# A fused Mamba2 and mixture-of-experts block: decays exponentiated in SBUF, channel tiles on alternating PSUM banks, output weights one slot sooner, a reordered end

## The reference

```
xn = layernorm(x)                                     # x: 1 x 1024 x 512
proj = xn @ in_proj_w.T                               # gate 8192 | hBC 10240 | dt 128
hBC  = silu(causal_conv4(hBC) + conv_b)               # hs 8192 | B 8 x 128 | C 8 x 128
dt   = clip(softplus(dt + dt_bias), 0, 100); A = -exp(A_log)
# 128 heads of 64 channels, 8 chunks of 128 tokens, A_cum = cumsum(dt * A) in a chunk
L    = exp(segsum(dt * A))                            # 128 x 128 lower triangle, a head and a chunk
Y_diag = (C B^T * L) @ (hs * dt)                      # inside a chunk
state  = decay * state + B^T @ (decay_states * hs * dt)
Y_off  = (C @ previous state) * exp(A_cum)
g    = (Y_diag + Y_off + hs * D) * silu(gate)
out  = (g * rsqrt(mean(g * g, group of 1024) + 1e-5) * norm_w) @ out_proj_w.T
result = x + out + x @ base_W.T + LoRA experts (top 2 of 8 by softmax)
```

## Time and profile before

| | |
|---|---|
| median of 3 runs | 1668.06 us (1667.99 to 1668.83) |
| profiled execution | 1670.87 us, span 1669.3 us |
| mean granted TensorE clock | 0.991 |
| busy, TensorE matmuls | 1616.3 us |
| busy, VectorE / ScalarE / POOL | 1366.4 / 1243.0 / 1327.1 us |

### The profile page before, as it was taken

How to read it: one execution, slowest core, us unless ns; L and a number is a source line. 1 busy time by engine, 2 the same in 40 slices (tenths; PEclk the granted TensorE clock), 3 DMA queues, 4 the chain that set the end, 5 groups by cost and what they waited for, 6 DMA issues and landing times.

```text
span 1669.3 us, 31876 instructions
## 1 busy us (share of the span) xinstructions
PE 1616.3 (97%) x10792; PEld 1308.9 (78%) x10792; DVE 1366.4 (82%) x1675; ACT 1243.0 (74%) x2625; POOL 1327.1 (80%) x1238
## 2 busy tenths in 40 slices
PE   7989999999999999999999999999999999999998
PEld 5777887878788787878878787887878788787776
DVE  5868789877888888887888888888788877888777
ACT  5267787777778687777878778787777878777774
POOL 3147689987889778896899868998788977999886
PEclk9999999999999999999999999999999999999999
DMA  3153365454544554445545446554554446544453
GB/s 125 58 201 103 113 179 166 147 158 126 163 145 127 159 155 138 127 133 149 172 144 151 125 117 181 145 144 137 156 159 121 140 131 183 150 125 133 128 146 101
DMA packets 216401, 236.11 MB, mean 141 GB/s; under 512 B 154280, under 2 KB 155824, under 8 KB 212016
## 3 DMA queue, kind: packets, MB, share of 16 engines
q1 hardware_dynamic: 216240, 234.08, 48.1%
HBM read 147.52 MB, written 55.05 MB: 121 GB/s over the span
## 4 chain that ended last, share of the span: by engine, by line
PE 82%; DVE 8%; issue 4%; ACT 4%; POOL 2%; DMA 1%; ACTq 0%; DVEq 0%; SPq 0%; POOLq 0%
PE P L262 9%; PE P L264 9%; PE P L263 9%; PE P L499 8%; PE P L363 6%; PE P L339 6%; PE P L340 6%; PE P L356 6%; PE P L346 6%; PE P L357 6%; PE P L370 4%; DVE OL L836 3%; ACT OH L795 1%; PE P L489 1%; PE P L486 1%
## 5 line engine op out<-in xcount | busy, mean ns | idle before, releaser
L595 ACT ACTIVATE P<-AB,SC 128x128 f32<-128x128 f32 x1016 | 307.1, 362 | 25.3 <-DVE EM L926 25.1
L262 PE MATMUL P<-xh,AH 128*128 128x512 f32 x656 | 262.5, 400 | 3.5 <-DVE xl L957 2.9
L264 PE MATMUL P<-xh,AL 128*128 128x512 f32 x656 | 256.7, 391 | 0.0
L263 PE MATMUL P<-xl,AH 128*128 128x512 f32 x656 | 256.1, 390 | 0.0
L813 DVE SCALAR_TENSOR_TENSOR hsX<-P,cwt,hsX 128x1023 f32<-128x1023 f32 x189 | 241.8, 1279 | 13.1 <-ACT hsX L532 8.6
L339 PE MATMUL P<-GH,xh 128*128 128x512 f32 x512 | 215.3, 421 | 0.0
L356 PE MATMUL P<-OH,gTh 128*128 128x512 f32 x512 | 201.4, 393 | 2.9 <-issue 2.7
L340 PE MATMUL P<-GH,xl 128*128 128x512 f32 x512 | 203.6, 398 | 0.0
L357 PE MATMUL P<-OH,gTl 128*128 128x512 f32 x512 | 200.1, 391 | 0.0
L1249 POOL TENSOR_TENSOR al<-al,dhs 128x512 f32<-128x512 f32 x64 | 97.4, 1522 | 113.2 <-DVE al L1093 113.2
L926 DVE TENSOR_TENSOR EM<-P,Gt 128x1024 f32<-128x1024 f32 x127 | 154.7, 1218 | 23.6 <-issue 22.1
(11 more groups left out here) (223 smaller groups left out, 4158.7 us busy)
## 6 DMA issues: line engine op xcount, KB each, us to landing
AB<-acr_d SPq DMA_DIRECT2D x128, 512.0 KB, 4.6
half_d<-hsX SPq DMA_DIRECT2D x60, 512.0 KB, 3.4
AR<-in_wa SPq DMA_DIRECT2D x80, 256.0 KB, 2.7
TS<-in_wg SPq DMA_DIRECT2D x16, 1024.0 KB, 6.4
TS<-in_wo SPq DMA_DIRECT2D x16, 1024.0 KB, 6.4
part_d<-pl SPq DMA_DIRECT2D x64, 256.0 KB, 3.1
pl<-part_d SPq DMA_DIRECT2D x64, 256.0 KB, 3.5
SC<-sct_d SPq DMA_DIRECT2D x16, 128.0 KB, 5.3
```

What stands on the lines that cost most here:

```text
L262: te.matmul(o, ah_, bh_, start=(first and i == 0), stop=False)
L263: te.matmul(o, ah_, bl_, start=False, stop=False)
L264: r = te.matmul(o, al_, bh_, start=False, stop=(last and i == n - 1))
L595: r = se.activation(decays(m)[:, h, :], AB[m % 2][:, h, :], ACT.Relu, bias=SC[s % 2][:, c, 3, h:h + 1], scale=-1.0)
```

## The change

1. `E` goes. The relus and the exponential write `EM[m % 2]` in SBUF, and the decay product works in place, `EM <- EM, Gt`, with both inputs in SBUF. The relus of m+1 wait for Y(m-1), which frees the buffer, where they waited for the product of m; the product no longer has a wait of its own for Y.
2. Channel tiles take banks (0, 1) and (2, 3) in turn.
3. At c = 1 ScalarE makes the four `OH` ahead of `gTh`, not behind it; VectorE makes the three low output weights at the end of the slot c = 1, ahead of `gTl`, not in slot c = 2; POOL makes the fourth behind its front work of c = 1. The next load into `TS` is issued at c = 2, not c = 3.
4. In the last slot Off(127) comes ahead of O(125). The last gated chunk is transposed into four banks; its high and low parts are made 128 columns at a time (3 more instructions on ScalarE and on VectorE), and the last output goes k by k, three matmuls for each, into bank 4; O(126) takes bank 1.

```diff
-        jobs += [("A", k // 2, (0, 1))] if k % 2 == 0 else []
+        jobs += [("A", k // 2, ((0, 1), (2, 3))[k // 2 % 2])] if k % 2 == 0 else []
...
-            jobs += [("O", m - 2, (4,)), ("GTr", m - 1, (5,))] if m == M - 1 else []
             jobs += [("Off", m, (0 if spare else 5,))] if c else []
             jobs += [("St", m, (1 if spare else 6,))] if c != 7 else []
-            jobs += [("O", m - 2, (4,))] if 2 <= m < M - 1 else []
+            jobs += [("O", m - 2, (4,))] if m >= 2 else []
+            jobs += [("GTr", m - 1, (5,))] if m == M - 1 else []
...
-            jobs += [("O", m - 1, (4,)), ("GTr", m, (5,)), ("O", m, (1,))] if m == M - 1 else []
+            jobs += [("O", m - 1, (1,)), ("GTr", m, (5, 6, 2, 3)), ("O", m, (4,))] if m == M - 1 else []
...
-        E = P[:, 2:4, :].rearrange("p b (h l) -> p (b h) l", h=4)
...
         def decays(m):
-            return E[:, :, :] if m else EM[0][:, :].rearrange("p (h l) -> p h l", h=8)
+            return EM[m % 2][:, :].rearrange("p (h l) -> p h l", h=8)
...
             pe_output(M - 2)
             pe_turn_gated(M - 1)
-            pe_output(M - 1)
+            banks_free("O", M - 1)
+            o = bank("O", M - 1)
+            for k in range(4):
+                te.wait_ge(s_gth, M + k)
+                te.matmul(o, gTh[:, k, :], OH[:, k, :], start=k == 0, stop=False)
+                te.matmul(o, gTh[:, k, :], OL[:, k, :], start=False, stop=False)
+                te.wait_ge(s_gtl, M + k)
+                r = te.matmul(o, gTl[:, k, :], OH[:, k, :], start=False, stop=k == 3)
+            r.then_inc(s_o, 1)
...
-            if m:
-                se.wait_ge(s_m, m)
-            else:
+            if m > 1:
+                se.wait_ge(s_y, m - 1)
+            elif m == 0:
                 se.wait_ge(s_ac, NC)
             if m == 1:
-                se.wait_ge(s_conv, 18)
+                se.wait_ge(s_x, 6)
             for h in range(8):
                 r = se.activation(decays(m)[:, h, :], AB[m % 2][:, h, :], ACT.Relu, bias=SC[s % 2][:, c, 3, h:h + 1], scale=-1.0)
...
-                if m:
-                    act_gated_hi(m - 1)
                 if m < M and c == 1:
...
                         se.activation(OH[:, j, :], TS[:, j, :], ACT.Copy, scale=nwt[:, 4 * s + j:4 * s + j + 1]).then_inc(s_oh, 1)
+                if m:
+                    act_gated_hi(m - 1)
...
             ve.wait_ge(s_exp, m + 1)
-            if m > 1:
-                ve.wait_ge(s_y, m - 1)
-            ve.tensor_tensor(EM[m % 2][:, :].rearrange("p (h l) -> p h l", h=8), decays(m),
+            ve.tensor_tensor(decays(m), decays(m),
                              Gt[:, c, :].unsqueeze(1).broadcast_to([128, 8, 128]), ALU.mult).then_inc(s_m, 1)
...
-                if m < M and c == 2:
-                    dve_output_lo(s, (0, 1))
...
-                if m < M and c == 2:
-                    dve_output_lo(s, (2,))
...
                 if m < M:
                     dve_sum(m)
                     dve_gated(m)
+                if m < M and c == 1:
+                    dve_output_lo(s, (0, 1, 2))
                 if m and m != M - 1 and m <= M:
                     dve_gated_lo(m - 1)
...
-                    if c == 3 and s + 1 < NS:
+                    if c == 2 and s + 1 < NS:
                         sp.wait_ge(s_ol, 3 * s + 3)
```

More of the change, by code:

```diff
@@ L64, in mamba_moe_block_kernel @@
         if m == 0:
-            jobs += [("A", k // 2, (0, 1)) for k in slot_halves[1] if k % 2 == 0]
+            jobs += [("A", k // 2, ((0, 1), (2, 3))[k // 2 % 2]) for k in slot_halves[1] if k % 2 == 0]
         if m + 1 < M:
@@ L69, in mamba_moe_block_kernel @@
         if m < M:
-            jobs += [("A", k // 2, (0, 1)) for k in slot_halves[m + 1] if k % 2 == 0 and m]
+            jobs += [("A", k // 2, ((0, 1), (2, 3))[k // 2 % 2]) for k in slot_halves[m + 1] if k % 2 == 0 and m]
             spare = not any(slot_halves[n] for n in range(m, M + 1))
-            jobs += [("O", m - 2, (4,)), ("GTr", m - 1, (5,))] if m == M - 1 else []
             jobs += [("Off", m, (0 if spare else 5,))] if c else []
             jobs += [("St", m, (1 if spare else 6,))] if c != 7 else []
-            jobs += [("O", m - 2, (4,))] if 2 <= m < M - 1 else []
+            jobs += [("O", m - 2, (4,))] if m >= 2 else []
+            jobs += [("GTr", m - 1, (5,))] if m == M - 1 else []
             jobs += [("Y", m, (7,))]
@@ L245, in bank, with last_turned @@
             return P[:, at[kind, i][0], :]
+        def last_turned(k):
+            return P[:, at["GTr", M - 1][k], 0:128]
         def pair(kind, i):
@@ L369, in pe_turn_gated @@
             for t_ in range(4):
-                r = te.transpose(bank("GTr", m)[:, t_ * 128:(t_ + 1) * 128], gated[m % 2][:, t_ * 128:(t_ + 1) * 128], ident[:, :])
+                o = bank("GTr", m)[:, t_ * 128:(t_ + 1) * 128] if m < M - 1 else last_turned(t_)
+                r = te.transpose(o, gated[m % 2][:, t_ * 128:(t_ + 1) * 128], ident[:, :])
             r.then_inc(s_gtr, 1)
@@ L468, in pe_program @@
                     pe_front(1)
-                if m == M - 1:
-                    pe_output(m - 2)
-                    pe_turn_gated(m - 1)
                 if c:
@@ L489, in pe_program @@
                     te.matmul(o, BH[:, c, :], DL[:, :], start=False, stop=True).then_inc(s_stp, 1)
-                if 2 <= m < M - 1:
+                if m >= 2:
                     pe_output(m - 2)
+                if m == M - 1:
+                    pe_turn_gated(m - 1)
                 banks_free("Y", m)
@@ L620, in act_gated_hi @@
                 se.wait_ge(s_o, m)
-            se.activation(gTh[:, :, :], bank("GTr", m).rearrange("p (k t) -> p k t", k=4), ACT.Copy).then_inc(s_gth, 1)
+            if m < M - 1:
+                se.activation(gTh[:, :, :], bank("GTr", m).rearrange("p (k t) -> p k t", k=4), ACT.Copy).then_inc(s_gth, 1)
+            else:
+                for k in range(4):
+                    se.activation(gTh[:, k, :], last_turned(k), ACT.Copy).then_inc(s_gth, 1)
         def act_square(m):
@@ L851, in dve_gated_lo @@
             ve.wait_ge(s_gth, m + 1)
-            ve.tensor_tensor(gTl[:, :, :], bank("GTr", m).rearrange("p (k t) -> p k t", k=4),
-                             as_f(gTh[:, :, :]), ALU.subtract).then_inc(s_gtl, 1)
+            if m < M - 1:
+                ve.tensor_tensor(gTl[:, :, :], bank("GTr", m).rearrange("p (k t) -> p k t", k=4),
+                                 as_f(gTh[:, :, :]), ALU.subtract).then_inc(s_gtl, 1)
+            else:
+                for k in range(4):
+                    ve.wait_ge(s_gth, M + k)
+                    ve.tensor_tensor(gTl[:, k, :], last_turned(k), as_f(gTh[:, k, :]), ALU.subtract).then_inc(s_gtl, 1)
         def dve_output(m):
@@ L1082, in dve_program @@
                         dve_silu(i)
-                if m < M and c == 2:
-                    dve_output_lo(s, (0, 1))
-                if m == M - 1:
-                    dve_output(m - 2)
-                    dve_gated_lo(m - 1)
                 if m < M and c:
@@ L1113, in dve_program @@
                         dve_silu(i)
-                if m >= 2 and m != M - 1:
+                if m >= 2:
                     dve_output(m - 2)
+                if m == M - 1:
+                    dve_gated_lo(m - 1)
                 if m < M:
@@ L1230, in pool_program @@
                 s, c = divmod(m, 8)
-                if m < M and c == 2:
-                    pe_.wait_ge(s_oh, 4 * s + 1)
-                    pe_.tensor_tensor(OL[:, 3, :], TS[:, 3, :], as_f(OH[:, 3, :]), ALU.subtract).then_inc(s_olp, 1)
                 if m + 1 < M:
@@ L1251, in pool_program @@
                         pool_front(m + 1)
+                    if c == 1:
+                        pe_.wait_ge(s_oh, 4 * s + 1)
+                        pe_.tensor_tensor(OL[:, 3, :], TS[:, 3, :], as_f(OH[:, 3, :]), ALU.subtract).then_inc(s_olp, 1)
                     for k in slot_halves[m]:
```

## The result

The changed kernel takes 1685.88 us (median of 4 runs, 1684.0 to 1687.23) against 1668.44 us for the kernel before (4 runs): 1.010 times as long, 95% interval 1.0083 to 1.0118. It is slower by some 17 us. The profiled execution has a span of 1685.9 us, 16.6 more than before, and a mean granted clock of 0.994, where before it was 0.991.

The account below looks back on a forecast made before the run. TensorE, at work 97% of the span, was taken to set the time, waiting mainly for low output weights. Terms -0.6 + 3.5 + 7.7 + 0.1 + 2.2 - 3.5 = +9.4 us on 1668.06 gave 1677, range 1672 to 1688.

Parts of the forecast that it names:

- What a SBUF input costs: Each of 127 decay products: +0.5 us on VectorE, +1.0 us on POOL where POOL runs without idle.
- Nothing of that is on TensorE's path where slots have slack: Decays in SBUF: the products' longer times add nothing to TensorE's time, except at three places counted separately.
- Low weights, even groups: Even groups 2 to 14, around slot 65: POOL's lag makes 3.8 us of new stall replace 2.7; +7.7 us in all.
- rival A: Idle time covers the ports' price, so the stalls shrink: 1647 us, or 1639 if half-clock stretches go too; chance 0.35.
- Low weights, odd groups: Seven odd groups, as in slot 58: the 1.1 us wait goes, St stalls 1.6 us for the gate; +3.5 us in all.
- The last group: Slots from 122 on: POOL's slot becomes 9.7 us, +5.5; the stall of slot 122 goes, -3.3; net +2.2 us.
- The end: After the last Y: the last 12 matmuls start 0.5 us after the transposes and finish sooner; -3.5 us.
- Banks: Channel tiles' banks in turn: removes TensorE's one wait of 0.6 us; -0.6 us.
- Rival B: Gains and losses cancel as the stalls change place: 1665 to 1671 us; chance 0.14.
- Rival C: POOL becomes the bound outside the boundaries, 0.5 us in 40 more slots, +20: 1697 us; chance 0.08.

Follow-up runs that it names:

- e3: Kernel before, with only the product's input moved: exponential writes EM in SBUF, product in place there, relus still in PSUM; 1697.62 us, ratio 1.0181.
- e4: Kernel before, with relus writing EM in SBUF and waiting for Y, exponential writing PSUM and the product reading PSUM; 1668.69 us, ratio 1.0002.
- e8: As e3, but the exponential writes the relus' input buffer in SBUF; the product reads that and writes EM, not in place; 1699.78 us, ratio 1.0177.
- e2_end: Kernel before with the fourth part of the change alone (the end reordered); 1666.17 us, ratio 0.9989.
- e12: Changed kernel without its second part: all channel tiles in banks 0 and 1; 1684.7 us, ratio to the kernel before 1.0109.
- e1_weights: Kernel before with the third part alone (output weights at c = 1, ahead of gTl), decays in PSUM; 1649.67 us, ratio 0.9887.

## Why the prediction was right in sign and range, and where it failed

The forecast was 1677 us, from 1672 to 1688, and 1685.88 came: 17.4 us more than before by the medians, where 9.4 were worked out. The mechanism was right, and so was the price of one product. That the number lies in the range is in part luck: 12.3 us at slots that were put at nothing stand against 5.8 us at slots that were put at nothing too, and 4.3 us too many in a third place.

- **What a SBUF input costs.** Right. VectorE was to lose 0.5 us a product and lost 0.57 (1791 - 1218); POOL 1.0, and it lost 138 us in 128 slots, 1.08. e3, e4 and e8 show that it is the second SBUF input and nothing else. The stricter rule of the page "SBUF — State Buffer" of the Trainium skill, section "Who interferes with whom", an exclusive lock that the one that comes first keeps for its whole instruction, was set aside too soon. The large neighbours on POOL lose 1.0 (2.28 - 1.28, the last group) and 0.9 (2.17 - 1.28, slot 57), less than a product's 1.22 us. But the two small ones of slot 63 end 0.05 us after VectorE's instruction does, and where the product comes first, as at 808.41 us, it takes its 1216 ns with POOL beside it. Both are as that rule has it, with the later one losing what is left of the other's instruction when it starts.
- **"Nothing of that is on TensorE's path where slots have slack".** This step failed, and with it the size. I had looked at the slack of the gate ahead of St in the slots with c = 2 and taken the rest for granted. The slots with c = 6 and 7 of the odd groups cost 12.3 us, through another wait: VectorE evicts `Gt` from the bank of the output product, and POOL's small instructions, which I left at their old length, hold up VectorE ahead of it. e3 shows the same 12 us (3.7 + 8.5) with only the product's input moved.
- **"Low weights, even groups", +7.7.** Mis-sized: +3.4 at c = 1, 0.4 to 0.9 a group where 1.1 was worked out. The lag of POOL was to gather over three products and arrive whole at slot 65. Part of it is paid at slot 63 instead, which loses 1.2 us a group, and the next sum comes 3.5 us after its Y began, not 5 (931.7 less 926.7, where that Y began before). Slot 65 of the changed kernel, VectorE and TensorE:

```profile
939.58 0.70 DVE L901 TENSOR_TENSOR P<-P,al 128x512 f32<-128x512 f32 x1 [0.51 <-POOL al L1260]
...
940.92 3.96 DVE L850 SCALAR_TENSOR_TENSOR OL<-TS,nwt,OH 128x512 fp32r<-128x512 f32 x3
```

```profile
936.06 1.15 PE L501 MATMUL P<-xch,EM 128*64 128x64 f32 x32
...
945.53 0.50 PE L477 MATMUL P<-SH,CH 128*128 128x512 f32 x1 [1.87 <-DVE gTl L867]
...
948.03 0.50 PE L358 MATMUL P<-OH,gTh 128*128 128x512 f32 x1 [0.84 <-DVE Gt L921]
```

  Off still waits there, 1.87 us, and the output product 0.84, as much together as the 2.7 us that the low weights cost before. So the stall keeps its size and changes its name, and the lag was counted in the wrong place: here and at c = 6 and 7 of the odd groups 7.7 us were predicted together and 15.7 measured.
- **The clock.** The sum has no term for it outside the end; only rival A held that stretches at the lower level might go. Three of its five went, 4.7 us of the -5.8 at c = 2 of the even groups, though the stalls did not shrink. That was nothing the forecast had counted on. Without that the changed kernel would have been slower by some 21 us, not 17.
- **"Low weights, odd groups", +3.5.** Right in size (+3.1). The wait has another name: not St for the gate but Off for `gTl`, 0.7 us earlier in TensorE's list, through bank 5. I had not followed what `gTl` frees.
- **The last group**, +2.2: +3.5, with POOL's turn at 9.72 us where 9.7 was worked out; the 2.6 us of slot 119 had no term. **The end**, -3.5: -2.6, or -3.3 with the 0.7 us that e2_end shows in slot 126, which the table counts to the last group. The first matmul came 0.46 us after the transposes had ended, as worked out (0.5). The 1.6 us that hang on the clock came with it. **Banks**: nothing that can be measured (e12).
- **Rival A** (the ports' price is covered by idle time) fell with both its premises: a product was to lose 0.26 us and loses 0.57, a low weight was to take 1.0 us and takes 1.48. Its price for the third part comes near the truth only with the product left in PSUM (e1_weights, 18 us). **Rival B** (1665 to 1671) fell by the number. **Rival C** (POOL the bound outside the boundaries, +20) has something in it: the 12.3 us are such a place, but 14 slots at 0.9 us, not 40 at 0.5, and the wait is for `Gt`, neither for gated chunks nor for `DL`.

## What to carry to other kernels

Moving one input of an often repeated VectorE instruction from PSUM to SBUF can cost more than anything that the freed PSUM buys, when POOL is busy: here 30 us for 127 products. POOL's share of the loss put in by itself cost 17.5 us, VectorE's 7.7. Before such a move, look on both engines for what comes next to it in time, the shortest instructions too. And when a stalled step is moved ahead in a list, follow what every step that it passes frees (a bank, a buffer), not only who reads its result. Last, compare the granted clock stretch by stretch before a difference is put down to stalls: here each stretch at the lower level cost about 1.5 us, and they made a third of the third part's gain.

## What was not expected of the hardware

POOL instructions on one element per partition, 0.19 us in the kernel before, took 1.17 us beside a product with two SBUF inputs and 1.05 us beside the silu of VectorE. ScalarE's relus and exponential were a little slower into SBUF (395 ns against 362 for a relu; 1055 against 1013 for the exponential, of which e3_exp_sbuf, where only its output is in SBUF, shows 1020), which cost nothing here.
